# Counts turned by DMA instead of TensorE, with a new order of the first layer's selects and opening

## What is computed

```python
inter = xf @ c1_w.T @ c2_w.T                       # rank 16, 1792 columns
blk = inter.reshape(B * T, 56, 32)
idx = jnp.argmax(blk, axis=-1) + jnp.arange(0, INTER, SPARSITY)
h = relu(einsum('bkm,bm->bk', w1[idx], xf))
out = einsum('bk,bkm->bm', h, w2t[idx])
```

## Time and profile before

| | us |
|---|---|
| median of the runs (3) | 686.1 |
| lowest run | 684.95 |
| profiled execution | 688.99 |
| its span | 687.2 |
| TensorE busy | 652.9 |
| VectorE busy | 457.9 |
| GpSimd busy | 231.4 |
| ScalarE busy | 213.8 |

### The profile page before, as it was taken

One profiled execution on the slowest core, in us unless ns is written; L12 is line 12 of the kernel. 1 busy time (PEld: TensorE's weight loads), 2 busy tenths in 40 slices (PEclk: granted clock), 3 DMA queues, 4 the chain that ended last, 5 costly groups with the idle time before them and its releaser, 6 DMA issues.

```text
span 687.2 us, 8637 instructions
## 1 busy us (share of the span) xinstructions
PE 652.9 (95%) x3078; PEld 519.8 (76%) x3078; DVE 457.9 (67%) x716; ACT 213.8 (31%) x379; POOL 231.4 (34%) x185
## 2 busy tenths in 40 slices
PE   2599999999999999999999999889999999999997
PEld 2477777777777877777777777668878887887887
DVE  7877775596764596665596885675856576485643
ACT  3424333412122412222313134435136225413610
POOL 2416455460000450000570335435334152442441
PEclk9899999999999999999999999989999999999999
DMA  9940000040000040000062110040013014001101
GB/s 265 387 141 1 0 1 0 32 154 1 0 1 0 32 153 0 0 0 0 31 223 79 61 62 0 16 169 0 31 38 116 1 46 137 0 31 47 47 17 46
DMA packets 19535, 40.66 MB, mean 59 GB/s; under 512 B 2032, under 2 KB 2416, under 8 KB 18864
## 3 DMA queue, kind: packets, MB, share of 16 engines
q1 hardware_dynamic: 19504, 40.25, 16.9%
HBM read 31.85 MB, written 8.39 MB: 59 GB/s over the span
## 4 chain that ended last, share of the span: by engine, by line
PE 84%; DVE 11%; issue 4%; ACT 1%; POOL 0%; DVEq 0%; ACTq 0%
PE bank L405 74%; PE bank L339 2%; PE bank L1145 2%; DVE eq L863 2%; DVE seg_top L861 2%; PE bank L1108 1%; PE bank L1126 1%; DVE counts L873 1%; PE bank L1240 1%; PE bank L1277 1%; DVE h_lo L897 1%; DVE ws_lo L926 1%; DVE x_tile L379 1%; DVE h L888 0%; DVE ws_raw L921 0%
## 5 line engine op out<-in xcount | busy, mean ns | idle before, releaser
L405 PE MATMUL bank<-w_hi_t,h_hi 128*128 128x512 f32 x224 | 93.7, 418 | 1.7 <-DVE h_lo L897 1.7
L699 ACT ACTIVATE h_hi<-h 128x512 fp32r<-128x512 f32 x56 | 35.4, 632 | 182.8 <-DVE h L888 182.8
L873 DVE TENSOR_TENSOR_SCAN counts<-restart,eq 128x512 bf16<-128x512 bf16 (+1 forms) x64 | 88.2, 1378 | 2.0
L405 PE MATMUL bank<-xT_hi,w_hi_t 128*128 128x512 f32 x224 | 88.7, 396 | 0.0
L405 PE MATMUL bank<-w_hi_t,h_lo 128*128 128x512 f32 x224 | 88.5, 395 | 0.0
L405 PE MATMUL bank<-w_lo_t,h_hi 128*128 128x512 f32 x224 | 88.5, 395 | 0.0
L405 PE MATMUL bank<-xT_hi,w_lo_t 128*128 128x512 f32 x224 | 88.5, 395 | 0.0
L405 PE MATMUL bank<-xT_lo,w_hi_t 128*128 128x512 f32 x224 | 88.4, 395 | 0.0
L861 DVE TENSOR_REDUCE seg_top<-bank 128x16 f32<-128x512 f32 (+1 forms) x64 | 39.5, 617 | 72.1 <-PE bank L1126 72.1
L385 POOL TENSOR_TENSOR g_tile<-g_tile,s_tile 128x512 f32<-128x512 f32 x31 | 40.6, 1310 | 94.9 <-DVE g_tile L910 56.5
L613 POOL TENSOR_TENSOR prod_lo<-prod,prod_hi 128x512 fp32r<-128x512 f32 x32 | 40.7, 1293 | 70.9 <-ACT prod_hi L737 70.9
(11 more groups left out here) (185 smaller groups left out, 1326.1 us busy)
## 6 DMA issues: line engine op xcount, KB each, us to landing
w_raw<-in_w SPq DMA_DIRECT2D x28, 256.0 KB, 10.1
x_res<-in_x SPq DMA_DIRECT2D x4, 1024.0 KB, 8.4
mid_state<-g_tile SPq DMA_DIRECT2D x16, 256.0 KB, 2.1
x_tile<-mid_state SPq DMA_DIRECT2D x4, 1024.0 KB, 7.6
x_res<-mid_state SPq DMA_DIRECT2D x4, 1024.0 KB, 5.5
out<-g_tile SPq DMA_DIRECT2D x15, 256.0 KB, 2.0
x_tile<-in_x SPq DMA_DIRECT2D x3, 1024.0 KB, 5.3
b_raw<-in_lora_b SPq DMA_DIRECT2D x2, 1024.0 KB, 4.8
```

The costliest lines, as they stand in the source:

```text
L405: last = nc.tensor.matmul(dst, a, b, start=(start and n == 0), stop=(stop and n == len(mms) - 1))
L699: nc.scalar.activation(h_hi[:, it % 2, :], h[:], ACT.Copy).then_inc(h_hi_done, 1)
L873: nc.vector.tensor_tensor_scan(counts[:, p % 2, tt, 0:PW[p]], restart[:, 0:PW[p]], eq[:, 0:PW[p]], 0.0, ALU.mult, ALU.add).then_inc(sel_co ...
```

## The change

Pieces are 256, 512, 512 and 512 columns. TensorE no longer transposes counts: for each select SyncE waits for the scan and issues a transposing DMA from `counts` to `first`, which lies in SBUF now, double by piece (`turn`). The mask of the first slice of a piece waits for its four turns. The two banks that are free hold selects in turn (`sels`), so a select waits for the comparison two selects before. A head starts with selects; the rank product of the next chunk moves to the middle of the last down product, and t is rounded and split ahead of tanh and silu. h has two buffers, and ScalarE applies relu one iteration ahead. The row stores of a chunk are issued in the next chunk, between turns. GpSimd makes the four gate products before the four sums. The epsilon is added on VectorE. In the opening x comes in four tiles, each normalised when it is there, TensorE runs dummy matmuls on `restart` before and between the row transposes, and the mask's counts, the masked s weights and the s products lie in iterations 3 to 11 of the first chunk.

```diff
     PIECES = -(-INTER // BANK)
-    PW = [min(BANK, INTER - p * BANK) for p in range(PIECES)]
+    PW = [INTER - BANK * (PIECES - 1)] + [BANK] * (PIECES - 1)
+    PO = [sum(PW[:p]) for p in range(PIECES)]
+    AT = [(p, j) for p in range(PIECES) for j in range(PW[p] // P)]
...
-        counts = span_t.take("counts", [P, 2, TT, BANK], BF16)
+        first = span_t.take("first", [P, 2, TT, S], BF16)
+        counts = span_t.take("counts", [P, TT, BANK], BF16)
         seg_top = span_t.take("seg_top", [P, BANK // SEG])
-        h = span_t.take("h", [P, S])
-        before_h = Span(span_t.end)
...
+            for tt in range(TT + 1):
+                if tt < TT:
+                    dve.wait_ge(ld_x if tt == TT - 1 else ld_x_first[tt], 16)
+                    nc.vector.bn_stats(bn[:, tt, :], x_tile[:, tt, :]).then_inc(stats_in, 1)
+                    dve.wait_ge(stats_in, tt + 1)
+                    nc.vector.bn_aggr(mean_var[:, tt, :], bn[:, tt, :]).then_inc(stats, 1)
+                    dve.wait_ge(stats, tt + 1)
+                    nc.vector.tensor_scalar(mean_var[:, tt, 1:2], mean_var[:, tt, 1:2], EPS, None, ALU.add)\
+                        .then_inc(var_eps, 1)
+                if tt:
+                    dve.wait_ge(rstd_done, tt)
+                    rows_scale(tt - 1)
...
-        first = banks[7][:].bitcast(BF16)[:, 0:S]
+        sels = [banks[6], banks[7]]
...
+        WARM = 14
+        WS_AT = (5, 6)
+        MASK_N = TT * NEXT[WS_AT[0] - 1][0] + NEXT[WS_AT[0] - 1][1]
+        S_AT = (9, 11)
...
+            def turn(c, p, tt):
+                sp.wait_ge(sel_count, c * NSEL + p * TT + tt + 1)
+                sp.sem_inc(turns, 1)
+                sp.dma_start_transpose(first[:, p % 2, 0:PW[p] // P, rows(tt)], counts[:, tt, 0:PW[p]])\
+                    .then_inc(ld_first[tt], 16)
+            def weights(it):
+                if it < IT:
+                    sp.dma_start(w1_raw[:, it], w1[it]).then_inc(ld_w1[it], 16)
...
+            sp.dma_start(c1_nat[:], c1_w).then_inc(ld_c1, 16)
+            for tt in range(TT):
+                sp.dma_start(x_tile[:, tt, :], x_rows[0][:, tt, :]).then_inc(ld_x if tt == TT - 1 else ld_x_first[tt], 16)
+            weights(0)
+            weights(1)
             sp.wait_ge(c2_zero, 1)
...
                 sp.dma_start(c2_f[q * Q:q * Q + RANK, :], c2_w).then_inc(ld_c2, 16)
-            sp.dma_start(w1_raw[:, 0], w1[0]).then_inc(ld_w1[0], 16)
+            for it in range(2, 5):
+                weights(it)
+            sp.dma_start(mask_nat[:], mask).then_inc(ld_mask, 16)
             sp.dma_start(ws_raw[:], w_s0).then_inc(ld_ws0, 16)
-            sp.dma_start(w1_raw[:, 1], w1[1]).then_inc(ld_w1[1], 16)
-            for it in range(2, IT + 2):
-                if it < IT:
-                    sp.dma_start(w1_raw[:, it], w1[it]).then_inc(ld_w1[it], 16)
...
+                turn(0, 0, tt)
+            weights(5)
+            turn(0, 1, 0)
+            turn(0, 1, 1)
+            weights(6)
...
+            def chunk(c, source, place, last):
+                for tt in range(TT):
+                    turn(c, 0, tt)
+                store_rows(c - 1, place)
+                for tt in range(2):
+                    turn(c, 1, tt)
+                sp.wait_ge(st_rows, c * TT * 16)
+                sp.sem_inc(g_free, 1)
+                for n in range(2):
+                    turn(c, *NEXT[n])
                 sp.wait_ge(xT_tr, c * TT + TT)
                 sp.dma_start(x_tile[:], source).then_inc(ld_x, 16)
                 sp.dma_start(x_res[:], x_rows[c]).then_inc(ld_res, 16)
...
+                    if it == IT - 1:
+                        for tt in range(2):
+                            rows_hi(act, c + 1, tt)
+                    elif it + 1 >= begun:
+                        relu(c, it + 1)
...
+                if not last:
+                    t_round(c + 1)
...
+                for tt in range(2):
+                    select(c, 1, tt)
...
+                    todo = [(1, 2 * it), (1, 2 * it + 1)] if opening and it < 2 else NEXT[it:it + 1]
                     dve.wait_ge(relu_done, c * IT + it + 1)
-                    dve.wait_ge(first_tr, c * IT + it + 1)
-                    nc.vector.scalar_tensor_tensor(h[:], first, 1.0, h[:], ALU.is_equal, ALU.mult).then_inc(h_masked, 1)
+                    p, j = AT[it]
+                    if j == 0:
+                        for tt in range(TT):
+                            dve.wait_ge(ld_first[tt], (c * PIECES + p + 1) * 16)
+                    nc.vector.scalar_tensor_tensor(h[:, it % 2, :], first[:, p % 2, j, :], 1.0, h[:, it % 2, :],
...
+                    if opening and it == WS_AT[0] - 1:
+                        mask_switch()
+                    if todo:
+                        select_largest(c, *todo[0])
...
+                    if opening:
+                        if it == WS_AT[0] - 2:
+                            mask_counts()
+                        if it == WS_AT[0] - 1:
+                            mask_ws(range(0, 2))
+                        if it == WS_AT[0]:
+                            mask_ws(range(2, 4))
+                        if it in (WS_AT[0] + 1, WS_AT[0] + 2):
+                            ws_rest(range(2 * (it - WS_AT[0] - 1), 2 * (it - WS_AT[0] - 1) + 2))
+                for tt in range(2, TT):
                     rows_lo(dve, c + 1, tt)
+                if not last:
+                    t_rest(c + 1)
...
+                n = p * TT + tt
+                if n == 0:
                     pe.wait_ge(t_split, c + 1)
...
+                elif n >= 2:
+                    pe.wait_ge(sel_eq, c * NSEL + n - 1)
+                nc.tensor.matmul(sels[n % 2][:, 0:PW[p]], t_stack[:, rows(tt)],
+                                 c2_stack[:, PO[p]:PO[p] + PW[p]], start=True, stop=True).then_inc(sel_done, 1)
...
-            def transpose_counts(c, it):
-                pe.wait_ge(sel_count, c * NSEL + (it // 4 + 1) * TT)
-                if it:
-                    pe.wait_ge(h_masked, c * IT + it)
-                for tt in range(TT):
-                    last = nc.tensor.transpose(first[:, rows(tt)], counts[:, it // 4 % 2, tt, rows(it % 4)], ident_bf[:])
-                last.then_inc(first_tr, 1)
...
+                select(c, 0, 0)
+                select(c, 0, 1)
                 s_product(c, 0)
+                select(c, 0, 2)
+                select(c, 0, 3)
                 s_product(c, 1)
-                select(c, 0, 0)
+                select(c, 1, 0)
+                select(c, 1, 1)
                 s_product(c, 2)
-                select(c, 0, 1)
                 s_product(c, 3)
-                select(c, 0, 2)
...
+                up_product(c, 0)
+            def first_chunk(it):
+                if it == 1:
+                    select(0, 0, 2)
+                    select(0, 0, 3)
+                elif it < 4:
+                    if it == 2:
+                        pe.wait_ge(c2_split, 2)
+                    select(0, 1, 2 * (it - 2))
+                    select(0, 1, 2 * (it - 2) + 1)
+                elif it <= len(NEXT):
+                    if it - 1 == WS_AT[0] - 1:
+                        pe.wait_ge(seg_in, 5)
+                        pe.wait_ge(mask_sum, 1)
+                        pe.wait_ge(sel_eq, MASK_N - 1)
+                        nc.tensor.matmul(sels[MASK_N % 2][:, 0:KD * MB], seg_ones, row_cnt[:, 0:KD * MB],
+                                         start=True, stop=True).then_inc(mask_cnt, 1)
+                        pe.wait_ge(mask_on, 1)
+                    select(0, *NEXT[it - 1])
+            def body(c, first, last):
+                for it in range(1, IT):
+                    if first and it in S_AT:
+                        s_product(0, 2 * S_AT.index(it))
+                        s_product(0, 2 * S_AT.index(it) + 1)
+                    if first and it - 1 in S_AT:
+                        pe.wait_ge(s0_read, 2 * S_AT.index(it - 1) + 2)
+                    elif first and it in S_AT:
+                        pe.wait_ge(s0_read, 2 * S_AT.index(it) + 1)
+                    up_product(c, it)
+                    if first:
+                        first_chunk(it)
+                    elif it <= len(NEXT):
+                        select(c, *NEXT[it - 1])
                     if it >= 2:
                         pe.wait_ge(h_split, c * IT + it - 1)
-                        if first and it == 2:
-                            pe.wait_ge(s0_read, TT)
                         down_product(it - 2, range(TT)).then_inc(down_done, 1)
+                        if first and it == 3:
+                            select(0, *NEXT[2])
...
+                pe.wait_ge(h_split, c * IT + IT - 1)
+                down_product(IT - 2, range(TT)).then_inc(down_done, 1)
                 pe.wait_ge(h_split, c * IT + IT)
                 down_product(IT - 1, range(0, 2))
-                pe.wait_ge(xT_done, (c + 1) * TT + 2)
-                transpose_rows(pe, c + 1, 3)
```

(11 more changed lines are left out.)

444 lines of the change are left out of this document (229 added, 215 removed).

## The result

| kernel | median of runs | lowest to highest | span of the profiled execution | rank product of chunks 1, 2, 3 starts at |
|---|---|---|---|---|
| before | 686.35 us | 684.95 to 686.6, but for one of 2580 | 687.2 | 128.99, 231.14, 333.27 |
| changed | 706.2 us | 702.89 to 706.62 | 704.5 | 147.13, 249.78, 352.35 |

The account below looks back on a forecast made before the run. TensorE, busy 95%, was taken to bound the kernel, with VectorE's chain setting the changed opening. Opening chunk +3.1 us and three later chunks -3.3 gave -0.2 against the 687.2 span: 686 us, range 668 to 704.

Parts of the forecast that it names:

- Count transposes leave TensorE: Every chunk: 14 groups of four transposes at .28 us leave TensorE, saving 3.9 us a chunk, 15.7 in all four.
- A turn takes 3.0 us: Scan end to mask start, through the transposing DMA: 3.0 us, ends 1.7 and 5.3; costs nothing in chunks 1 to 3.
- The rival with the long turn: Turns above 3.0 us delay the opening, longer ones the other chunks; at 6.0 us +15, giving 701; chance 0.2.
- The estimate of 5.2 us: Turn of four 128x128 blocks one after another at the skill's 1309 ns each; the sum would end near 694.
- Order at a head: Heads of chunks 1 to 3: TensorE waits 1.0, 1.8 and 0.8 us for comparisons, 3.6 us together, lower end 2.4.
- The opening, start: Chunk 0: rank product starts at 13.3 instead of 16.29 and ends at 15.2, not 20.05; 4.9 us won.
- The opening, VectorE's chain to 83.6: Chunk 0: VectorE's selections, iterations, mask work and turn waits run as one chain from 27.1 to 83.6, up to the masked s product.
- GpSimd's stretching: Opening chain: GpSimd's weight splitting stretches ten scans by 0.3 us and part of ws_lo, 5.2 us, ends 0 and 9.
- From the s product to the end of the next rank product: 50.6 us: Chunk 0's end on TensorE: 7.3 for slow s products, 31.3 for 134 matmuls, 12.0 to the end, at 134.2.
- At nothing: Parts priced at no cost: relu ahead with two h buffers, later row scaling, epsilon on VectorE, gate order, second layer.
- The range's ends: VectorE's chain alone: lower ends 73.6 giving 671.5, upper 94.4 giving 699; whole range 668 to 704.
- the first mechanism: VectorE's chain sets the opening, TensorE idle some 20 us there; 686 us, chance 0.55.

Follow-up runs that it names:

- both orders: Changed kernel; GpSimd takes standard deviations before the last remainders and bias adds in chunk 0, TensorE s products 0 and 1 before selections 2 and 3 in heads; 686.21 us.
- the filled pause: Changed kernel with eight matmuls of ones ahead of the waiting selection in the heads of chunks 1 to 3, no wait shortened; 701.58 us, ratio 1.0206.
- the turns done twice: Changed kernel with standard deviations early on GpSimd and s products 0, 1 ahead of selections 2, 3 in heads, plus each piece's last turn done twice; 702.46 us.
- the order of a head: Changed kernel with s products of row tiles 0 and 1 ahead of selections of row tiles 2 and 3 in chunks 1 to 3; 690.78 us, ratio 1.0064.
- the standard deviations first: Changed kernel; in chunk 0 GpSimd takes chunk 1's reciprocal standard deviations ahead of the last two weight remainders and four bias adds; 694.18 us, ratio 1.0107.
- GpSimd idle: Changed kernel with standard deviations early on GpSimd, and chunk 0's w1, w2 remainders replaced by rounded copies on ScalarE; 680.39 us, ratio .9886.

## Why the prediction was wrong, step by step

- **Count transposes leave TensorE.** They do. The price of a group, .28 us from one pair of rows, holds where TensorE bounds (.30 by the iterations with both orders), and the chunks 1 to 3 then came out 4 to 5.5 us shorter, for 4.7 in the sum. In chunk 0 it doesn't show. Doing the transposes twice cost .23 us a group and 9 us in all; taking work out and putting it in did not weigh the same.
- **A turn takes 3.0 us.** It took 2.4, inside the ends of 1.7 and 5.3 from the earlier trace rows. Up to the s product VectorE waited for one turn, 2.63 us, where the sum had three, 5.0. That it is free in the middle chunks was right: with the last turn of each piece later by 2.4 us or more these chunks grew by 1.2 us, the two together. The rival with the long turn is out. The estimate of 5.2 us, worked out from the Trainium skill, "VectorE: DVE Perf Modes", section The three transpose paths, is out too: a turn of four blocks took less than half of it.
- **Order at a head: 1.0 + 1.8 + .8 us.** .69 + 2.19 came, and no third, since the second and third s product give selections 4 and 5 time enough. The mechanism was right and its sum, 2.88 for 3.6, too. What failed is that I priced the pause and stopped: the earlier trace rows had shown a slow matmul behind a pause of 3.29 us, and I used that for the opening and not for the heads. The 12 matmuls behind it cost 2.3 us more, in the middle chunks 2.6 by the filled pause. A period of 101.1 was forecast, 102.6 came, and 100.0 where the clock held.
- **The opening, start.** Rank product at 13.3, done at 15.2: 13.14 and 15.24 came.
- **The opening, VectorE's chain to 83.6.** It ended at 90.24. The mis-sized term is GpSimd's stretching. I took the mean of all 512-wide scans, of which most run while GpSimd is idle, and gave ten of them .3 us: 5.2 with the weights' share. Measured: 13 instructions, 13.5 us; the splits of h and a mask product are among them, which I had left unstretched. The earlier trace rows held both kinds, 1.22 and 2.22 us; it was one or the other by what GpSimd did at the time, and from 15 to 90 us it subtracts through 30.37 of 75 us. The term was 8.3 us too small. VectorE waited 4.4 us for selections' matmuls, where the sum had 2.4, and 2.6 for turns, where it had 5.0. The other terms, together, came 1.3 us shorter, which leaves the 6.6 by which the chain came late. The upper end of the term, 9, did not reach 13.5 either.
- **From the s product to the end of the next rank product: 50.6 us.** 60.1 came (90.24 to 150.37). Of the 9.5 us, 7.54 are the pause for the standard deviations, and 1.50 the slow clock behind it (the sixteen transposes took 3.41 us, those of the next two chunks 1.91). This step failed outright: the sum has TensorE's work alone and puts the standard deviations at nothing. I followed what the new opening puts on VectorE and TensorE, listed for SyncE what queues behind its new waits, and did not do it for ScalarE and GpSimd. ScalarE's last rounding of w2 now comes an iteration later, and GpSimd's last remainder, the bias adds and the standard deviations with it.
- **At nothing.** Of the terms put at nothing the standard deviations cost something, as above, and so does the mask product that reads SBUF now. The second layer's code is as it was; its 1.1 us are a difference between two executions.
- **The last chunk** was to gain 1.1 us like the two before it, and gained .7. It has waits of its own (1.84 us ahead of its row transposes, and 8.9 us more with the turns done twice), and it should have had a line of its own.
- **The range's ends.** Two are added up wrongly. The lower end of the chain, 73.6, starts from 25.5 us for which no row stands, and is 10.0 below 83.6, which is 6.9 us less in chunk 0 and not 7.6. The upper one, 94.4, is 10.8 above it; with the heads as in the sum that gives 697, not 699. Neither changes where 706 lies.

The rivals: none of them is what happened. The result is the first mechanism (VectorE's chain; TensorE's pauses from 27 to 90 us are 20.2 us together, as its sum had them) with 16.1 us more up to the end of the next rank product, of which 9.5 are not of that mechanism, and with 1.5 us more than forecast in each middle chunk. The rival on the slow side, a long turn, gave nearly the right time for a reason that is not there.

## What to carry to other kernels

When work is moved to a later place, follow for every engine what waits for it, and what stands behind that waiter in its own list. Here a rounding of .62 us was put one iteration later on ScalarE; GpSimd's list waited for it, with a step of 1 us at its end, and that held TensorE for 7.5. Price VectorE's instructions by rows taken while GpSimd does what it will do in the new place, not by a mean. And in front of an instruction that waits, put work that doesn't (the order of a head: 15 us for two lines); filling the pause with idle matmuls gets back only the clock, and only where TensorE is what bounds the stretch.

## What the runs showed of the hardware

- A DMA that turns counts from one place in SBUF to another (48 of 128x512 bf16, 16 of 128x256) landed 2.4 us after its issue (2.3 at least, 7.9 at most) and held the issuing queue for 1.19 us, where the issue of a plain load held it for .40 to .78. The narrow ones took about as long as the wide ones (2.3 and 2.4 us).
- VectorE's instructions that read two tiles in SBUF (the scan, the split of h, the mask product) ran up to 1.1 us longer when a subtraction of GpSimd was under way (2.3 us for 1.22, the same scan). Those that took one of them from a bank did not (the comparison, .69 us either way), nor did the counting of the mask, which reads one (2.25 and 2.26).
- The same pause of 2.18 us on TensorE was followed by 1.2 GHz in six heads of six of the changed kernel's two traces, in none of two with the standard deviations first, and in one of three (2.18 to 2.25 us) with GpSimd idle. Behind the lower clock the 12 matmuls of 512 columns cost .427 us each and not .233.
